# Macaron block on one core: new waits and positions for the indirect transfers, the last sum and two weight copies

## What is computed

```
x = x + 0.5 * ffn(layernorm(x))
x = x + attn(layernorm(x))
x = x + 0.5 * ffn(layernorm(x))

attn(x): xc = x - mean over the 512 tokens, per head
         corr = softmax(xc @ xc.T);  out = corr @ x
ffn(x):  w, idx = top_k(softmax(x @ Wg + bg), 2);  w = w / sum(w)
         h = relu(x @ W1[e] + b1[e]);  y = h @ W2[e] + b2[e]
         out = sum over the two chosen experts of w * y
```

## Time and profile before

| | us |
|---|---|
| median of 3 runs (1116.67 to 1118.45) | 1118.09 |
| the profiled execution | 1119.98 |
| its span, first to last instruction | 1118.2 |
| TensorE matmul busy | 1049.5 (94%) |
| VectorE (DVE) busy | 849.1 (76%) |
| ScalarE (ACT) busy | 826.4 (74%) |
| GpSimd (POOL) busy | 525.7 (47%) |

### The profile page before, as it was taken

The page is one execution under the profiler, slowest core; times in us unless marked ns, Lnnn a source line. Parts: engine busy times, 40 slices in busy tenths (PEclk is TensorE's granted clock), DMA queues, the critical chain, the costliest instruction groups (busy, mean ns, idle before and its releaser), DMA issues.

```text
span 1118.2 us, 20894 instructions
## 1 busy us (share of the span) xinstructions
PE 1049.5 (94%) x6817; PEld 608.1 (54%) x6817; DVE 849.1 (76%) x2315; ACT 826.4 (74%) x1124; POOL 525.7 (47%) x562
## 2 busy tenths in 40 slices
PE   4999999989999998998999999999899999999996
PEld 2777778723333326884322232233258877777784
DVE  6889899956767766774677777677458769999986
ACT  4444454379999997897989998999899964455441
POOL 5454457543444350002455665654300007878885
PEclk9899999989999998999999999999999999999998
DMA  7332223100000333432001111115114612334431
GB/s 200 146 118 114 77 85 120 48 16 15 18 20 18 96 102 106 142 132 73 24 29 32 37 32 34 34 34 171 50 59 140 218 66 101 117 126 157 160 122 54
DMA packets 56831, 96.25 MB, mean 86 GB/s; under 512 B 7819, under 2 KB 28435, under 8 KB 56723
## 3 DMA queue, kind: packets, MB, share of 16 engines
q1 hardware_dynamic: 47298, 76.83, 20.5%
q0 software_dynamic: 8192, 16.79, 4.8%
q10 hardware_dynamic: 1234, 1.29, 0.3%
HBM read 61.60 MB, written 33.29 MB: 85 GB/s over the span
## 4 chain that ended last, share of the span: by engine, by line
PE 69%; ACT 16%; issue 7%; DVE 4%; POOL 2%; DMA 1%; SPq 1%; ACTq 0%; POOLq 0%; DVEq 0%
PE ps L1539 11%; ACT probs L1755 10%; PE ps L1524 6%; PE ps L615 5%; PE ps L617 5%; PE ps L616 5%; PE ps L631 5%; PE ps L632 5%; PE ps L636 5%; ACT sums L1755 5%; PE ps L1187 2%; PE ps L1189 2%; PE ps L1188 2%; PE ps L1173 2%; PE ps L1198 2%
## 5 line engine op out<-in xcount | busy, mean ns | idle before, releaser
L1755 ACT ACTIVATE probs<-ps 128x1024 f32<-128x1024 f32 x344 | 335.7, 1111 | 22.1 <-PE ps L1524 20.7
L1003 ACT ACTIVATE high<-ps 128x512 fp32r<-128x512 f32 x256 | 153.2, 600 | 139.5 <-PE ps L617 125.6
L1468 POOL DMA_INDIRECT sorted<-xn,slot x128 | 128.9, 1007 | 160.2 <-ACT probs L1755 83.0
L1480 POOL DMA_INDIRECT found<-tiles,home x128 | 126.3, 987 | 138.2 <-ACT sums L1755 105.3
L1074 POOL TENSOR_TENSOR sums<-sums 128x512 f32<-128x512 f32 x112 | 144.9, 1294 | 95.0 <-DVE sums L865 93.4
L1539 PE MATMUL ps<-probs,value 128*32 128x512 f32 x1376 | 188.3, 620 | 1.1 <-DVE mixed L1665 0.4
L1755 ACT ACTIVATE sums<-ps 128x1024 f32<-128x1024 f32 x168 | 173.0, 1112 | 13.4 <-PE ps L1524 12.9
L842 DVE SCALAR_TENSOR_TENSOR low<-ps,high 128x512 fp32r<-128x512 f32 x256 | 163.7, 680 | 21.4 <-ACT high L1003 19.8
L1524 PE MATMUL ps<-shared 32*128 32x512 f16 x1024 | 142.2, 389 | 25.0 <-ACT probs L1755 8.3
L1524 PEld LDWEIGHTS ps<-shared 32*128 32x128 f16 x1024 | 37.8, 91 | 155.4 <-ACT probs L1755 75.7
L615 PE MATMUL ps<-xh,weights 128*128 128x512 f32 x256 | 109.3, 427 | 0.0
(11 more groups left out here) (181 smaller groups left out, 1888.6 us busy)
## 6 DMA issues: line engine op xcount, KB each, us to landing
wide<-gates SPq DMA_DIRECT2D x32, 512.0 KB
probs<-gates SPq DMA_DIRECT2D x32, 512.0 KB, 4.0
found<-sorted SPq DMA_DIRECT2D x46, 256.0 KB, 2.6
tiles<-sums SPq DMA_DIRECT2D x46, 256.0 KB, 2.0
sorted<-zeros SPq DMA_DIRECT2D x16, 512.0 KB
out<-X SPq DMA_DIRECT2D x16, 256.0 KB
X<-in_L_attn_x SPq DMA_DIRECT2D x3, 1024.0 KB, 9.4
sorted<-xn,slot POOLq DMA_INDIRECT x128
```

Source lines behind the costliest of these rows:

```text
L1003: nc.scalar.activation(high[:, third(m), c, :], ps[:, hidden_bank(m, c), :], ACT.Relu).then_inc(sm["f_high"], 1)
L1755: nc.scalar.activation(ring[ring_at(n)], ps[:, score_banks(n), :], ACT.Exp, scale=SCORE).then_inc(sm["a_probs"], 1)
```

## The change

- During attention every indirect transfer has a count of its own from a list: `PACE` for ordinary sequences, `SENDS_OF_RUSH` for `s` = 6 and 15, `FIRST_COLLECTS` for the first eight collects. The eight sends of the early sorted sequence, of which three stood in whole job 7, all stand in `s` = 0. POOL's small work stands at fixed places among the 16 positions of a sequence.
- In the last stage nine collects are issued for each whole job instead of eight (two in slot 1), so that they end in slot 0 of job 15, and VectorE's 16 `combine_half` stand at the places of `ADDED`, the last in slot 4 of job 15.
- The very last `total_up` is done by VectorE.
- At the start of a stream the weights of tiles 0 and 1 are copied one after the other, in the first stream ahead of the first `x_high`, in the second behind it; tile 2's follow one position earlier than before.
- The order of two stores near the end is swapped.

```diff
@@ -49,6 +49,16 @@
+PACE = 2, 4, 7, 8, 10, 12, 13, 16, 17, 20, 22, 24, 26, 27, 30, 32
+SENDS_OF_RUSH = (2, 3, 4, 5, 6, 7, 12, 13), (2, 4, 6, 8, 10, 12, 14, 16)
+FIRST_COLLECTS = 16, 17, 19, 20, 22, 23, 25, 26
+RATE = E + 1
+ADDED = {(1, 2): 0, (1, 4): 1, (2, 2): 2, (2, 4): 3, (3, 0): 4, (3, 2): 5, (3, 5): 6, (4, 0): 7, (4, 4): 8, (4, 5): 9,
+         (5, 4): 10, (5, 5): 11, (6, 4): 12, (6, 5): 13, (7, 2): 14, (7, 4): 15}
@@ -682,8 +692,6 @@
-            if n == WHOLE - 1 and early_at(n - 2) is not None and e >= 5:
-                send(pool, early_at(n - 2), e - 5)
@@ -937,16 +945,15 @@
-                    if WHOLE < n <= WHOLE + NJOB:
-                        if e == 2:
-                            combine_half(dve, NJOB + n - WHOLE - 1, 0)
-                        if e == 5:
-                            combine_half(dve, NJOB + n - WHOLE - 1, 1)
-                if n == JOBS - 1:
-                    combine_half(dve, SORTED - 1, 0)
+                    if (n - WHOLE, e) in ADDED:
+                        at = ADDED[n - WHOLE, e]
+                        combine_half(dve, NJOB + at // TOPK, at % TOPK)
             scale(last * E - 1)
             if last == JOBS:
-                combine_half(dve, SORTED - 1, 1)
+                m = last * E - 1
+                dve.wait_ge(sm["f_scaled"], m + 1)
+                dve.wait_ge(sm["f_summed"], JOBS * (E - 1) - 1)
+                nc.vector.tensor_tensor(acc[:, side(JOBS - 1), :], acc[:, side(JOBS - 1), :], part[:, (E - 1) % 2, :], ALU.add).then_inc(sm["f_summed"], 1)
@@ -1086,12 +1093,11 @@
-                    if WHOLE <= n < JOBS - 1:
-                        collect(pool, NJOB + n - WHOLE, e)
...
+                    if n >= WHOLE:
+                        c = (n - WHOLE) * RATE + e + (e > 1)
+                        for at in (range(c, c + 2) if e == 1 else range(c, c + 1)):
+                            if at < NJOB * TOPK * J:
+                                collect(pool, NJOB + at // (TOPK * J), at % (TOPK * J))
@@ -1108,7 +1114,8 @@
-            total_up(last * E - 1)
+            if last < JOBS:
+                total_up(last * E - 1)
@@ -1447,11 +1454,19 @@
             for i in stream(a, b):
+                if i == a - 2 and a == 0:
+                    choose(a)
+                    choose(a + 1)
                 if in_stream(i + 2, a, b):
                     x_high(i + 2)
+                if i == a - 2 and a > 0:
+                    choose(a)
+                    choose(a + 1)
                 if in_stream(i + 1, a, b):
                     relu(i + 1)
-                if in_stream(i + 2, a, b):
+                if i == a - 1:
+                    choose(a + 2)
+                if i > a and in_stream(i + 2, a, b):
                     choose(i + 2)
@@ -1781,49 +1796,44 @@
-                if earlier is not None and (earlier + 1) % NJOB == 0 and hg < 2:
-                    sends = [[0], [1, 2], [3], [4, 5]] if hg == 0 else [[6], [7], [], []]
...
-                    for n in collects[k]:
-                        reached(pool, sm["a_probs"], g * UNITS + 2 * k)
-                        collect(pool, taking, n)
+        def attn_gpsimd(pool, s, half):
+            earlier = job_at(s - 1)
+            if s == 0:
+                earlier = early_at(WHOLE - 3)
+            more = s + 1 < S
+            q = s + 2 - WHOLE
+            first = s * G * UNITS
+            for i in range(8 * half, 8 * half + 8):
+                if i == 2 and more:
+                    norm_pool(pool, "a_", s + 1, (s + 1) % 2)
+                if i == 7 and more:
+                    attn_square_rows(pool, s + 1)
+                if i == 9 and more:
+                    attn_values(pool, s + 1)
+                if i == 14 and job_at(s + 1) is not None:
+                    norm_pool(pool, "r_", job_at(s + 1), job_at(s + 1) % 2)
+                if s in RUSH:
+                    if half == 0:
+                        pool.wait_ge(sm["a_probs"], first + SENDS_OF_RUSH[RUSH.index(s)][i])
+                        send(pool, earlier, i)
+                elif earlier is not None and i % 2 == 0:
+                    pool.wait_ge(sm["a_probs"], first + PACE[i])
+                    send(pool, earlier, i // 2)
+                if q == 0 and half == 1:
+                    pool.wait_ge(sm["a_probs"], first + FIRST_COLLECTS[i - 8])
+                    collect(pool, 0, i - 8)
...
+                if 1 < q < NJOB and i % 2 == 1 and i < 12:
+                    pool.wait_ge(sm["a_probs"], first + PACE[i])
+                    collect(pool, q, i // 2 + 2)
+                if 0 < q < NJOB - 1 and i in (13, 15):
+                    pool.wait_ge(sm["a_probs"], first + PACE[i])
+                    collect(pool, q + 1, i // 2 - 6)
```

More of the change, by code:

```diff
@@ L492, in _ @@
                     store_sorted(NJOB + n - WHOLE - 2)
+            store_sorted(SORTED - 2)
             store_whole(JOBS - 2)
-            store_sorted(SORTED - 2)
             store_sorted(SORTED - 1)
@@ L1088, in ffn_gpsimd @@
                         total_up(m - 1)
-                    if WHOLE <= n < JOBS - 1:
-                        collect(pool, NJOB + n - WHOLE, e)
-                    if n == JOBS - 2 and e >= 6:
-                        collect(pool, SORTED - 1, e - 6)
-                    if n == JOBS - 1 and e < 6:
-                        collect(pool, SORTED - 1, e + 2)
+                    if n >= WHOLE:
[3 more added lines that the diff above has]
+                                collect(pool, NJOB + at // (TOPK * J), at % (TOPK * J))
                     if n < WHOLE:
@@ new lines, in attn_gpsimd @@
+        def attn_gpsimd(pool, s, half):
[24 more added lines that the diff above has]
+                    collect(pool, 0, i - 8)
+                if q == 1 and i in (0, 1, 2, 3, 5, 7, 9, 11):
+                    pool.wait_ge(sm["a_probs"], first + PACE[i])
+                    collect(pool, 1, i if i < 4 else i // 2 + 2)
+                if 1 < q < NJOB and i % 2 == 1 and i < 12:
+                    pool.wait_ge(sm["a_probs"], first + PACE[i])
+                    collect(pool, q, i // 2 + 2)
+                if 0 < q < NJOB - 1 and i in (13, 15):
+                    pool.wait_ge(sm["a_probs"], first + PACE[i])
+                    collect(pool, q + 1, i // 2 - 6)
@@ L1843, in _ @@
             ffn_gpsimd(pool, 0, WHOLE)
-            attn_gpsimd(pool, 0, PAUSE)
-            attn_gpsimd(pool, PAUSE, S * G)
+            for half in range(2 * S):
+                attn_gpsimd(pool, half // 2, half % 2)
             norm_pool(pool, "f_", WHOLE, side(WHOLE))
```

38 lines of the change are left out of this document (removed).

## The result

The changed kernel takes 1103.26 us (median of 4 runs, 1103.02 to 1103.4), the kernel before beside it 1117.38 us (4 runs, 1115.3 to 1118.45). The ratio is 0.9876, 95% interval [0.9859, 0.9893]; the medians are 14.1 us apart. Forecast were 1098.5 us and a range of 1093 to 1110.

What follows compares the result with a forecast made beforehand. ScalarE's exponentials were taken to bound attention, TensorE the last stage's whole jobs. -13.4 - 3.5 + 4.0 - 1.8 - 2.5 + 0 - 2.4 = -19.6 us gave 1098.5 us, range 1093 to 1110.

Steps and rivals of the forecast that it cites:

- the pairs: Sequences 8 to 13: transfers two together at counts 12, 13 and 16, 17, taken to cost ScalarE nothing, as in sequence 14.
- Spacing, -13.4: Sequences 8 to 13: spaced transfers win back 13.4 of the 16.2 us lost, five sixths; bounds all or none.
- chain of nearly three: Sequences 8 to 13: close transfers still left behind the norm, the reason for taking only five sixths of 16.2 us.
- the wait grows with the length of the chain: Attention: ScalarE's wait for TensorE rises over one, two, four, seven back-to-back transfers; called a correlation, not a cause shown.
- Sequence 15, -3.5: Sequence 15: sends 1.86 us apart form no chain, so ScalarE's 3.5 us of waits go; bounds -3.5 and 0.
- Sequence 6, +4.0: Sequence 6: the eighth send, now behind the squares, delays the first stream's load by 4.0 us; bounds +3.3 and +4.7.
- Weights of two tiles, -1.8: Both streams: early copies remove TensorE's waits of 0.92 and 0.93 us for the second tile's weights; bounds 0 and -1.9.
- Job 7, -2.5: Job 7 to attention: without two sends the last sum starts 2.3 us earlier, clock may add; -2.5, between -2.0 and -3.5.
- Collects and halves, 0: Last stage: an extra transfer per job and three halves in two jobs cost nothing; bounds 0 and +1.2 us.
- Sequence 7, 0: Sequence 7 of attention: no change in its time was predicted, 0 us.
- The end, -2.4: Program's end: earlier scaling and the last sum on VectorE at 0.7 us save 2.4 us; bounds -1.8 and -2.9.
- transfers have nothing to do with it: Rival on TensorE's lateness in attention: ScalarE's waits stay, only the passages count, -2.7 us, 1115.4 us; chance 0.09.

Runs made afterwards that it cites:

- the undone counts: The changed kernel with PACE set back to 0, 2, 4, ..., 30, all other parts still changed: 1118.6 us, ratio 0.9942.
- the control: The changed kernel itself, unaltered, timed once more on the chip of the runs that followed: 1103.5 us, ratio 0.9858.
- the two runs of probes in single sequences: The changed kernel with chained sends, GpSimd products or plain transfers put into single early attention sequences, at two places: 1102.1 and 1104.1 us, each run once.
- the fast version with 256 waits: The changed kernel with sequence 6's sends at counts 2 to 9, the last ahead of the squares, plus 256 waits heading TensorE's list: 1108.3 us, ratio 0.9847.

## Why the prediction came out as it did

The sum was -19.6 us and the spans show -16.7; the other 1.9 us of the 4.8 by which 1098.5 was too low come from the reference: I took the profiled execution of before to stand to its median as that of after would, and the one of after lies at its median. Two of the signs that the prediction named went against it: sequences 8 to 13 took 183.6 us, not under 181, and new waits do stand behind the pairs of transfers. In its range the prediction counts 15.8 us as the better end of the spacing, where its own bound is 16.2; that would move the lower end by 0.4 us.

*Spacing, -13.4.* Right in kind, and the undone counts show it; 10.7 came, of which some 2.7 by way of the clock, which the prediction has no term for. I had expected the "chain of nearly three" to keep a sixth, but it left 0.5 us of waits; the pairs, which I had taken for free from sequence 14, left 2.4. Beside the 3.8 us of waits the six sequences are 1.6 us longer than six at 29.7, which no wait of 0.15 us or more explains. The step that was wrong is the reason: "the wait grows with the length of the chain". It does not: six cost what four did, and four can cost nothing. What the runs show in its place is that TensorE is late where close transfers meet its turning of operands (154 of 172 turnings), and by how much differs at the same phase. What ScalarE then waits, 0 to 1.9 us, no run explains in full.

*Sequence 15, -3.5.* -4.0; no wait is left.

*Sequence 6, +4.0.* The late send was right in place, and undoing it gives back 3.0 to 3.8 us. That the stage came out near the sum is partly luck. A chain of four stayed in this sequence, at 1.80 and 1.08 us of waits, so that the squares came 1.7 us later in it than before. The first tile's transposes start 24.4 us into the sequence instead of 18.2, 6.2 us later; what follows them got 2.5 us shorter, of which 0.9 is the weights.

*Weights of two tiles, -1.8.* The waits are gone, and undoing brings back 0.92 us in the first stream and 1.1 in the second. That the second stream's stretch rose all the same is job 8: 26.2 us in this profile, with a mean granted clock of 0.62 in 4.5 us of it, and 24.7 in the control. It took 26.1 to 26.2 us in 4 of the 14 profiles and 24.7 in the others. It is not of the change.

*Job 7, -2.5.* The wait fell by 2.3 as worked out. The upper end of the bound, the clock, was right in kind and too small: sequence 0 changed by -4.2 us here, with a mean granted clock of 1.00 instead of 0.91, and by -2.7 in the control (33.5 us, 0.95).

*Collects and halves, 0.* The bound held: +1.0, in slot 4 of jobs 10 and 11, where TensorE waits 0.5 us for normalised rows. In job 10, with two halves, a half took 2.13 us instead of 1.3:

```profile
960.86 2.13 DVE L1387 SCALAR_TENSOR_TENSOR X<-found,gates_sorted,X 128x128 f32<-128x128 f32 x4
...
960.77 1.28 POOL L1081 TENSOR_TENSOR sums<-sums 128x512 f32<-128x512 f32 x1
```

POOL's sum had begun 0.09 us earlier. I had quoted the rule for this, for the end, and not applied it here.

*Sequence 7, 0.* +1.3, but not shown to be of the change. Where the granted clock was at half speed in a part of this sequence it took 31.6 to 33.0 us, in the kernel before with 256 more waits too (32.2). Where it was at full speed throughout it took 30.6 to 30.9, in three versions with the changed counts (the two runs of probes in single sequences and the fast version with 256 waits) as in the kernel before (30.8). The wait of 1.62 us for rows behind the collected ones was 1.33 before.

*The end, -2.4.* -3.4. The last sum waited 0.5 us longer than I had it, and the transposes at full clock gave back 0.5, which the prediction had left out; the last expert no longer starts late.

The rival "transfers have nothing to do with it" is out: moving the same sends within a clean sequence makes waits of up to 1.41 us. Their traffic alone is probably not it. Plain transfers of the same size cost nothing, from SP or from GpSimd, but only one group of four stood where sends are known to cost something. As far as that goes, the trace agrees with what the Trainium skill says in "SBUF — State Buffer", section SBUF: two separate sides, that DMA traffic and a compute engine do not slow each other. What makes TensorE late beside indirect transfers stays open: it is not the fetch of its program and not the chain's length or its phase alone. GpSimd was issuing the sends while TensorE turned its operands and had finished issuing the plain transfers before; whether it is this issuing that matters was not tried.

## What to carry to other kernels

Spacing indirect transfers gained 10.7 us where nobody waited for them, a quarter of it because TensorE's clock no longer fell behind the waits. Where something waits for the last of a group, that is worth more than the chain: 7.2 us here, by sending faster and ahead of the squares. Work that is put on an engine with room still needs its data there in time; halves that stood too early cost 4 and 17 us. Read a stage in two profiles before giving its change to the edit: sequence 0 and job 8 moved by 1.5 us between runs of one kernel, and sequence 7 by as much, with the clock.

## What was not expected of the hardware

- Beside indirect transfers 1.3 us apart TensorE is late without any wait in its own rows: ScalarE waits up to 1.93 us for it in the kernel before. It depends on where the transfers meet TensorE's work, and at the same phase it comes in one sequence and not in another.
- GpSimd products of 128x512 stretch VectorE's instructions with two SBUF inputs (0.69 to 1.53 us) and its 16-bit copy (0.29 to 1.02 us), and leave those that read PSUM alone (the products `normed<-ps,recip`, 0.49 us in both). The Trainium skill has the first in "SBUF — State Buffer", section Who interferes with whom, and the trace agrees.
- 256 waits for a semaphore long set put TensorE's first matmul off from 10.35 to 18.62 us. TensorE would have waited for VectorE until 10.35 us anyway, so they took at least 8.3 us, 32 ns each.
